# Routed tiles gathered in one row and normed once, the last keys projected among the maxima, and the routed rows normed and scattered in four pairs

## The reference

```python
x = x + jnp.tanh(g_xattn[0]) * _L0_xattn_ref(_layernorm(x, axis=-1), ctx_1024, ctx_1024, ...)
x = x + jnp.tanh(g_ffn[0])   * _L0_ffn_ref(_layernorm(x, axis=-1), ...)   # mixture of experts
x = x + jnp.tanh(g_xattn[1]) * _L1_xattn_ref(_layernorm(x, axis=-1), ctx_1024, ctx_1024, ...)
x = x + jnp.tanh(g_ffn[1])   * _L1_ffn_ref(_layernorm(x, axis=-1), ...)   # quantised gated MLP
```

## Time and profile before

| | |
|---|---|
| Median of 3 runs | 970.43 us (969.73 to 970.9) |
| The profiled execution | 971.64 us, of which the span from first to last instruction is 969.7 us |
| Busy in the span | TensorE 89%, VectorE 65%, ScalarE 51%, GpSimd 17% |
| Granted TensorE clock, mean | 0.944 of 2.4 GHz |

### The profile page before, as it was taken

How to read it: one execution, slowest core, us unless ns; L and a number is a source line. 1 busy time by engine, 2 the same in 40 slices (tenths; PEclk the granted TensorE clock), 3 DMA queues, 4 the chain that set the end, 5 groups by cost and what they waited for, 6 DMA issues and landing times.

```text
span 969.7 us, 13594 instructions
## 1 busy us (share of the span) xinstructions
PE 863.8 (89%) x4064; PEld 434.4 (45%) x4065; DVE 628.3 (65%) x1245; ACT 498.3 (51%) x659; POOL 160.6 (17%) x269
## 2 busy tenths in 40 slices
PE   6979999999967999999997489999999979994098
PEld 4532333333444666666664223333333554441087
DVE  5688888888651222222347788888888468598932
ACT  2635777777731111111233147777777684597650
POOL 1421011111164000000056022100003504000000
PEclk9998999999997999999999689999999989997589
DMA  9693666554264101011169553333330000000011
GB/s 283 195 244 93 172 165 166 164 164 126 89 207 139 34 29 33 31 33 32 33 216 259 145 154 78 79 78 78 77 78 2 1 1 0 1 0 0 0 38 50
DMA packets 71324, 91.37 MB, mean 94 GB/s; under 512 B 26086, under 2 KB 56934, under 8 KB 71270
## 3 DMA queue, kind: packets, MB, share of 16 engines
q1 hardware_dynamic: 63292, 67.69, 27.2%
q0 software_dynamic: 5584, 19.93, 6.1%
q10 hardware_dynamic: 2400, 3.15, 1.0%
HBM read 62.90 MB, written 27.44 MB: 93 GB/s over the span
## 4 chain that ended last, share of the span: by engine, by line
PE 78%; DVE 9%; SPq 3%; ACT 3%; issue 3%; DMA 2%; POOL 2%; DVEq 0%; ACTq 0%
PE PS L1782 12%; PE PS L1750 12%; PE PS L1771 11%; PE PS L1925 8%; PE PS L1947 8%; PE PS L2013 7%; PE PS L2031 5%; DVE MX L1313 2%; PE PS L1936 2%; PE PS L1713 2%; PE PS L1881 2%; PE PS L1699 2%; PE PS L1733 1%; POOL slot_rows L788 1%; PE PS L1796 1%
## 5 line engine op out<-in xcount | busy, mean ns | idle before, releaser
L1313 DVE TENSOR_REDUCE MX<-PS 128x1 f32<-128x512 f32 x512 | 321.0, 683 | 48.3 <-PE PS L1750 47.3
L922 ACT ACTIVATE Pt<-PS 128x1024 f32<-128x1024 f32 x256 | 248.5, 1021 | 113.0 <-PE PS L1771 113.0
L1750 PE MATMUL PS<-KSt,BIG 96*128 96x512 bf16 x512 | 180.0, 397 | 8.0 <-DVE MX L1313 6.4
L1771 PE MATMUL PS<-BIG,KSt 99*128 99x512 bf16 x512 | 152.8, 385 | 0.3 <-DMA BIG<-MR 0.3
L1782 PE MATMUL PS<-Pt,VS 128*17 128x512 f32 x1024 | 136.2, 598 | 0.0
L1750 PEld LDWEIGHTS PS<-KSt,BIG 96*128 96x128 bf16 x512 | 41.2, 99 | 155.2 <-DVE MX L1313 103.0
L1925 PE MATMUL PS<-BIG,KSt 128*128 x184 | 85.6, 609 | 0.6 <-issue 0.6
L1947 PE MATMUL PS<-BIG,Pt 128*128 x368 | 84.2, 382 | 1.2 <-DVE Pt L1423 1.1
L1423 DVE COPY Pt<-PS 128x512 f32<-128x512 f32 x46 | 29.7, 686 | 84.7 <-PE PS L1936 84.7
L2013 PE MATMUL PS<-KSt,BIG 128*128 128x512 f32 x192 | 83.2, 593 | 0.9 <-ACT BIG L1026 0.7
L1771 PEld LDWEIGHTS PS<-BIG,KSt 99*128 99x128 bf16 x512 | 50.4, 99 | 55.1 <-issue 3.1
(11 more groups left out here) (198 smaller groups left out, 1015.4 us busy)
## 6 DMA issues: line engine op xcount, KB each, us to landing
qk_parts<-BIG SPq DMA_DIRECT2D x64, 192.0 KB, 3.2
BIG<-in_w POOLq DMA_DIRECT2D x12, 1024.0 KB, 5.8
BIG<-qk_parts SPq DMA_DIRECT2D x32, 192.0 KB, 3.3
KSt<-qk_parts SPq DMA_DIRECT2D x32, 192.0 KB, 3.7
v_rows<-BIG SPq DMA_DIRECT2D x8, 544.0 KB, 4.6
VS<-v_rows SPq DMA_DIRECT2D x32, 136.0 KB, 2.9
BIG<-qk_parts SPq DMA_DIRECT2D x32, 128.0 KB, 3.8
KSt<-qk_parts SPq DMA_DIRECT2D x32, 128.0 KB, 3.9
```

What stands on the lines that cost most here:

```text
L922: act.activation(PP[:, 2 * (kc % 2) + half, :, :].rearrange("p h t -> p (h t)"), ST[half], ACT.Exp, scale=DK ** -0.5).then_inc(exp_done, 1)
L1313: dve.tensor_reduce(MX[:, g % 2, i % TB, i // TB:i // TB + 1], ring(i), AX.X, ALU.max, negate=True).then_inc(max_taken, 1)
L1750: pe.matmul(ring(i), QS[0:ROWS, g, h, qc * P:(qc + 1) * P], KS[0:ROWS, g, h, :], start=True, stop=True).then_inc(max_done, 1)
L1771: last = pe.matmul(ST[half][:, i * S:(i + 1) * S], KS[0:ROWS + PARTS, g, h, kc * P:(kc + 1) * P], QS[0:ROWS + PARTS, g, h, :], start=True, ...
```

## The change

On layer 1's prep: GpSimd issues all 16 gathers in one row, as soon as the experts' results are stored, and the low parts of layer 1's first two key blocks and first query block move to VectorE. VectorE combines all eight routed tiles among the rests and the values, takes one norm over the eight ("back"), and ScalarE writes the normalised tiles (`write_back`). In both layers the projection of the last keys (batch 3) moves from in front of the maxima into their block, its matmuls one at a time between the scores (`key_step`), so the block now has six rests. The last queries use the keys' part buffers (`slot`, `landed`), and SyncE's order follows. ScalarE's Sqrt is gone from every norm but the last two. At the start, the key weight's load goes from ScalarE's queue to SyncE's, the slots are counted before the first projection, and `route_tiles` stands between the first statistics. At the end of layer 0, the routed tiles are normed in four pairs.

```diff
-            def low_part(layer, kind, p):
+            def low_part(layer, kind, p, c):
...
@@ GpSimd @@
             def prep(layer):
-                low_part(layer, "k", 0)
-                if layer:
+                if layer == 0:
+                    low_parts(0, "k", 0)
+                    low_parts(0, "k", 1)
+                    low_parts(0, "q", 0)
+                else:
                     gp.wait_ge(ys_out[0], 16 * ((SLOT_TILES + 1) // 2))
                     gp.wait_ge(ys_out[1], 16 * (SLOT_TILES // 2))
-                    gather(0)
-                    gather(1)
-                low_part(layer, "k", 1)
...
+                    for i in range(ROUTED):
+                        gather(i)
+                low_parts(layer, "k", 2)
+                low_parts(layer, "q", 1)
+                low_parts(layer, "k", 3)
+                low_part(layer, "q", 2, 0)
                 split_max(B * layer, 0)
...
@@ ScalarE @@
+            def write_back():
+                act.wait_ge(back_shift, 1)
+                for i in NORM_TILES["back"]:
+                    act.activation(XN[:, i, :], X[:, i, :], ACT.Identity, scale=rstd[:, i:i + 1],
+                                   bias=shift[:, i:i + 1]).then_inc(xn_ready, 1)
...
@@ VectorE @@
+            def low_parts(layer, kind, p):
+                for c in range(KC):
+                    dve.wait_ge(mid_done, made(layer, kind, p, c) + 1)
+                    dve.tensor_tensor(part_of(kind, p, c, 2), RB[:, c, :], part_of(kind, p, c, 1),
+                                      ALU.subtract).then_inc(lo_done, 1)
+            def first_maxima(layer):
+                n0 = B * layer
+                dve.wait_ge(v_taken, 2 * (n0 + B))
+                dve.memset(PV, 0.0).then_inc(pv_zero, 1)
+                maxima(n0, 0, range(6))
+                rest_of(layer, "k", 3, 0)
+                maxima(n0, 0, range(6, 10))
+                rest_of(layer, "k", 3, 1)
+                maxima(n0, 0, range(10, 14))
+                rest_of(layer, "q", 2, 0)
...
@@ SyncE @@
             def prep(layer):
...
                 load_stack(layer, 0, 0)
                 store_values(layer, 2)
                 load_stack(layer, 0, 1)
                 store_parts(layer, "q", 1)
+                store_values(layer, 3)
+                load_stack(layer, 0, 2)
+                store_parts(layer, "k", 3)
...
@@ TensorE @@
             def prep(layer):
                 pe.wait_ge(ct_in[ORDER[layer][3]], 16 * (layer + 1))
-                project_keys(layer, 3)
                 project_values(layer, 3)
-                turn_x(layer, 2)
...
                 max_scores(n0, 0, range(2))
+                key_step(layer, 3, 0, 0)
+                max_scores(n0, 0, range(2, 4))
+                key_step(layer, 3, 0, 1)
...
@@ VectorE @@
+            def pair_begin(h):
+                dve.wait_ge(x_upd, 2 * h + 2)
+                link(dve, norm_stats(NORM_TILES[f"moe{h}"], f"moe{h}"))
+                root_begin(f"moe{h}")
+            def pair_end(h):
+                root_end(f"moe{h}")
+                moe_writes(f"moe{h}")
```

More of the change, by code:

```diff
@@ L469, in x_tile @@
             return TB * ORDER[layer][i // TB] + i % TB
[L471 to L474, removed]
+        NORMS = [("first0", range(2 * TB)), ("first1", range(2 * TB, NT)), *[(f"moe{h}", range(2 * h, 2 * h + 2)) for h in range(TB)], ("rest", range(ROUTED, NT)), ("back", range(ROUTED)),
+                 ("ffn_a", x_tiles(FFN_A)), ("ffn_b", x_tiles(FFN_B))]
+        NORM_NO = {"ffn_a": 0, "ffn_b": 1}
         NORM_TILES = dict(NORMS)
@@ L538, in prep @@
                 store_parts(layer, "k", 2)
-                for j in range(4):
-                    sp.wait_ge(part_out[j], 32 * (n0 + 1))
+                for c in range(KC):
+                    sp.wait_ge(part_out[slot("k", 0, c)], landed(layer, "k", 1))
+                    sp.wait_ge(part_out[slot("q", 0, c)], landed(layer, "q", 1))
                 load_stack(layer, 0, 0)
@@ L582, in attention @@
             def attention(layer):
-                for j in range(4):
-                    sp.wait_ge(part_out[j], 32 * B * (layer + 1))
+                for c in range(KC):
+                    sp.wait_ge(part_out[c], 32 * (B + 1) * (layer + 1))
+                    sp.wait_ge(part_out[KC + c], 32 * (B - 1) * (layer + 1))
                 sp.wait_ge(v_out, 16 * B * (layer + 1))
@@ L981, in _ @@
                 expert_tile(t // 2, t % 2, t)
-                if t == SLOT_TILES - 2:
-                    norm("rest")
             prep(1)
@@ L1404, in _ @@
             route_slots()
-            link(dve, norm_stats(NORM_TILES["first0"], "first0"))
+            route_ranks()
+            norm_stats(range(TB), "first0")
+            route_tiles()
+            link(dve, norm_stats(range(TB, 2 * TB), "first0"))
             dve.wait_ge(ab_in, AB_IN[0])
```

291 lines of the change are left out of this document (138 added, 153 removed).

## The result

| | before | changed |
|---|---|---|
| Median | 970.08 us (4 runs, 967.43 to 970.9) | 957.75 us (4 runs, 956.48 to 958.25) |
| Span of the profiled execution | 969.7 us | 956.4 us |
| Ratio, 95% interval | | 0.988, 0.9864 to 0.9896 |

The changed kernel is 12.3 us faster; 19.9 had been forecast, and 957.75 lies 0.75 above the range of 946 to 957. The spans of the two profiled executions differ by 13.3. The same window of the changed kernel, to hold against the earlier trace rows, shows that the empty stretch has been filled: TensorE is busy 24.3 of 30 us there instead of 14.6, at a clock of 0.89 instead of 0.62.

What follows compares the result with a forecast made beforehand. TensorE's idle stretches, widest around layer 1's maxima, were taken as the bound. Gains of 16.5 (layer 1), 2.4 (between layers) and 1.0 (layer 0) sum to 19.9 us: 951.7 for the execution, median 950.5, range 946 to 957.

Steps and rivals of the forecast that it cites:

- Layer 1's block, term of 26.0: Layer 1's block of maxima, first reduction to first attention matmul: 22.5 us without a stall, 3.5 allowed for slow TensorE, 26.0.
- Layer 1's start, term of 4.5: Start of layer 1's maxima: the first reduction comes at 530.7 us, 4.5 earlier than before.
- the other 26.1 give 527.7. I add 1 for the wait: Layer 1's start: VectorE's remaining 26.1 of 31.4 us end at 527.7, plus 1 for the landing's second half.
- Rival (a): Layer 1's start: low parts at GpSimd's price or held by gather issues; first reduction 533 to 536, time 953 to 956; 20%.
- the rule weighed: Layer 1's start: gather issues contend with VectorE's two-input instructions; six held low parts add 5.8 us, the sum becoming 14.1.
- rival (d): Layer 1's gathers: VectorE starves their issue; slower than before once issues are above 2.7 us apart, 977 at 3.1; 4%.
- (c): Layer 1's block keeps waits of its own, for shared part buffers or SyncE's order: 32 instead of 26, 956.5 us; 11%.
- Rival (b): Between the layers: SyncE's queue doesn't hold the slots' load; 3.8 us more gained, time 946.7; 9%.
- Layer 0's prep, term of 1.0 gained: Layer 0's prep: block of maxima 2.3 to 2.8 us shorter, start 1.7 later, so 1.0 gained; bounds -1 and +2.8.
- VectorE waited for x already ... that makes the first rests 1.4 later. I take 1.7 later for the start: Layer 0's start: key weight ahead of x, `route_tiles` 4.0 us and norm 3.1 delay the first rests 1.4, the block 1.7.
- 22.5 and 0.5 to spare: Layer 0's block of maxima: without its stalls it takes 22.5 us plus 0.5, against 25.3 before.
- Between the layers, term of 2.4: Between the layers: with scatters done earlier, SyncE's queue empties 2.4 us earlier, slots landing near 294.1; bounds 0 and 6.2.

Runs made afterwards that it cites:

- e6: The changed kernel with layer 1's low parts of the first keys on VectorE ahead of the first values instead of behind them: 955.03 us, ratio 0.9844.
- e4: The changed kernel with layer 1's norm of the combined tiles and its shift moved ahead of the second queries' rests: 956.99 us, ratio 0.987.
- e3: The changed kernel with SyncE loading the first two slot tiles ahead of the last two experts' second weights and layer 1's output weight: 953.78 us, ratio 0.9831.
- e1: The changed kernel with layer 0's key weight loaded at the head of ScalarE's queue again, not ahead of x on SyncE's: 954.6 us, ratio 0.9857.
- e5: The changed kernel with layer 0's two prep norms made as before, with ScalarE's square root: 958.45 us, ratio 0.9871.
- e8: The changed kernel with the routed tiles normed and scattered in two halves as before, instead of four pairs: 959.87 us, ratio 0.9897.

## Why the prediction was wrong

**Layer 1's block, term of 26.0: right.** From the first reduction (533.91) to L1817 (559.74) are 25.8 us. The first two pairs of projection rows took 1.91 again, as forecast. ScalarE's eight writes took 0.5 each and not 0.39, and hid all the same.

**Layer 1's start, term of 4.5: half.** From the first key matmul to the first reduction the kernel before took 46.6 us (488.56 to 535.20), the changed one 44.5: 2.15 gained. The sum of VectorE's work was close: its low parts took 0.64 to 0.74, its combines 0.48. The step that failed is "the other 26.1 give 527.7. I add 1 for the wait": it let VectorE run nearly without a gap from the second keys' rests on. The second half of the landing held it 1.87 and not 1, and a step later the queries' high part held it another 1.49, for TensorE had stood 3.44 us and then projected in part at 1.2 GHz (5.37 us instead of the 3.67 in e6). e6 shows that chain to be a cause: with it shortened, the start is 2.3 shorter. The norm took 4.5 and not the 3.1 and 1 that I allowed; e4 shows that GpSimd's low parts do that, and that it was no loss by itself, because the second chain (the third values' landing, put at 528.7 to 530.1) ended near 532 too. So chains that end within 2 us of each other set the start, and I had two of them: e4, which shortens one, brings nothing, and e6, which shortens what stands ahead of both, brings 2.3.

**Rival (a) and the rule weighed.** The first reduction came where rival (a) has it, 533 to 536 (533.91, or 533.05 less the 0.86 by which layer 1 began later), but not by its mechanism: the low parts took 0.64 to 0.74, not 1.2, and weren't held by the gathers' issue. Its time of 953 to 956 was passed as well, by what layer 0 lost. The rule of the Trainium skill that I weighed (page "SBUF — State Buffer", "Who interferes with whom") would have had them held; no row here shows that. The 0.62 and 3.1 us named with rival (d) are on that page of the Trainium skill the times of a whole transfer that GpSimd issues, alone and beside a VectorE copy, and not of an issue; no run here has that pair. Rivals (c) and (d) didn't come: the block took 25.8 and not 32, and the last of the 16 issues began at 513.5. Rival (b) is answered by e3: the slots take 6.8 us to land behind SyncE's weights and 2.1 ahead of them.

**Layer 0's prep, term of 1.0 gained: the sign was wrong,** and it is the largest miss. The failed step is "VectorE waited for x already ... that makes the first rests 1.4 later. I take 1.7 later for the start". I priced `route_tiles` and the norm, and nothing for x's own landing behind the weight. It came 3.0 later (11.38 against 8.35), the rests 2.9, the first reduction 5.0 (55.74 against 50.74). e1 gives back 2.65 to 3.1 of what layer 0 lost. Of the 2.4 that e1 leaves at the first reduction, SyncE's store of the third values has 1.5 (issued at 45.87 instead of 44.36) and its landing 0.7 (5.0 us instead of 4.3); e5 shows that the norm alone isn't the reason, and what is stays open.

The second step that failed there is "22.5 and 0.5 to spare": 23.0 for the block, where 24.5 came (55.74 to 80.21), against 25.3 before; not 2.3 or more were gained but 0.9, which is no more than the spread. I had counted TensorE's slow start for layer 1 and not for layer 0. With the third values' landing late and the keys' projection moved into the block, TensorE stood 5.46 us ahead of the first scores, its granted clock from 55.12 to 57.60 was 0.50, the first projection rows took 1.91 instead of 1.02, and VectorE waited 1.27 for the next scores. Before the change TensorE came to the block without a pause, at a clock of 1.00 from 50.27 to 53.30. What happened is what the prediction named as a sign against it: "if layer 0's start costs more than its block gives back".

**Between the layers, term of 2.4: the size came, in part by luck.** From the last output projection to layer 1's first key matmul it is 199.8 instead of 202.5 us, 2.6 less. All of it was put down to the pairs, but with halves e8 has 200.4: by the rows the pairs bring 0.6 to 1.1 of the 2.6, by the medians 2.1, and no run shows where the rest comes from. The account, SyncE's queue holding the slots, is shown by e3. That stretch begins later, though, since layer 0's loss is carried into it.

In sum: 3.4 earlier was forecast at layer 1's first key matmul and 0.9 later came, 4.3 of the miss (5.1 of it lost at layer 0's first attention matmul, 0.6 regained in the attention, which is within the spread, and 0.2 between the layers); 2.35 are the start of layer 1's maxima. Those are the 6.6 by which the two spans' difference fell short.

## What to carry to other kernels

A load put at the head of a queue delays everything behind it on that queue, and so must be priced by what waits there first, not by its own use. A sum of an engine's work is a lower bound for its time: add the chain of landings beside it. Where two chains end close together, expect a gain only from an edit that moves both, as e6 did and e4 did not. An idle of TensorE costs more than its length when the clock falls with it: 3.44 us of idle came with 1.7 more in the projection behind it, 7.32 with 2.2 more in the slots' first product.

## What the runs showed of the hardware

Small operations of VectorE can wait out GpSimd's. In the changed kernel GpSimd computes two low parts from 19.55 to 21.82, some 1.13 us each (its timeline above). VectorE's operation of 20.04 ends at 20.73, that of 20.76 at 21.84, just behind the ends of the first and the second low part (20.7 and 21.8); the next one of the same kind takes 0.17 again. The same pair, 0.68 and 1.08, stands at 527.79 and 528.50, and with the low parts moved both take 0.17 (e4). The Trainium skill (page "SBUF — State Buffer", section "Who interferes with whom") has `tensor_scalar` among the VectorE operations that can take the port pair which VectorE has in common with GpSimd, and says that of two operations that want it the later one blocks fully; the trace agrees, even for 128x8 elements.

The gathers' issue didn't hold VectorE: the eight combine operations beside it took 0.47 or 0.48 us. The other way round there is a small effect. The issue of 497.95, begun while VectorE computed two low parts (497.18 to 498.46), took 1.33 us, where the other 15 took 0.94 to 1.03; e3 and e4 have two such issues each, of 1.30 to 1.41, all begun within VectorE's low parts. Others begun so took 0.97 (the issue of 509.66), so what decides it isn't shown. The issues came 1.24 to 1.34 us apart, and 1.63 behind the slow one: far from rival (d)'s 2.7.
